# Second cross attention on one core: the next batch's context normalised, and the latent columns scaled, by ScalarE instead of VectorE

## The reference, cut to what matters

```python
def _L1_xattn_ref(x, latents, key_padding_mask, kv_gate, ...):   # x: context (4, 1601, 256), latents (4, 512, 256)
    x = layernorm(x, gamma_media, beta_media)
    latents = layernorm(latents, gamma_lat, beta_lat)
    kv = jnp.concatenate((x, latents * kv_gate), axis=1)         # 2113 rows
    q = (latents @ Wq).reshape(b, n, HEADS, DIM_HEAD)            # 8 heads of 64
    k = (kv @ Wk).reshape(b, f + n, HEADS, DIM_HEAD)
    v = (kv @ Wv).reshape(b, f + n, HEADS, DIM_HEAD)
    sim = jnp.einsum('bqhd,bkhd->bhqk', q * SCALE, k)
    sim = sim - jax.lax.stop_gradient(jnp.max(sim, axis=-1, keepdims=True))
    sim = jnp.where(valid_full[:, None, None, :], sim, NEG_INF)
    attn = jax.nn.softmax(sim, axis=-1)
    out = jnp.einsum('bhqk,bkhd->bqhd', attn, v).reshape(b, n, HEADS * DIM_HEAD)
    return out @ Wout
```

## Time and profile before

| | |
|---|---|
| median of 3 runs | 2505.41 us (2494.01 to 2506.86) |
| the profiled execution's own time | 2506.49 us |
| its span, first to last instruction | 2504.7 us |
| granted TensorE clock, mean over the span | 0.915 |
| busy: TensorE / VectorE / ScalarE / GpSimd | 2048.3 / 1663.0 / 1011.3 / 1016.6 us |

### The profile page before, as it was taken

One profiled execution on the slowest core, in us unless ns is written; L12 is line 12 of the kernel. 1 busy time (PEld: TensorE's weight loads), 2 busy tenths in 40 slices (PEclk: granted clock), 3 DMA queues, 4 the chain that ended last, 5 costly groups with the idle time before them and its releaser, 6 DMA issues. The chain is left out here.

```text
span 2504.7 us, 35270 instructions
## 1 busy us (share of the span) xinstructions
PE 2048.3 (82%) x12728; PEld 1418.6 (57%) x12728; DVE 1663.0 (66%) x2539; ACT 1011.3 (40%) x1662; POOL 1016.6 (41%) x720
## 2 busy tenths in 40 slices
PE   7888857785999944687889888997989997499993
PEld 4555646673344433455556555665656664499992
DVE  5687743343679997489778887888778886422223
ACT  3333210001222210465666566754766674133332
POOL 2232221221344443055456645754566664122221
PEclk9999968897999976789999899998999998699996
DMA  3110044201000000200000000000000000351113
GB/s 143 36 36 20 12 171 158 76 31 59 1 0 0 1 0 3 84 1 1 12 17 1 9 1 27 1 1 9 1 1 1 9 1 1 142 202 35 39 37 109
DMA packets 36455, 93.26 MB, mean 37 GB/s; under 512 B 5160, under 2 KB 24124, under 8 KB 31679
## 3 DMA queue, kind: packets, MB, share of 16 engines
q1 hardware_dynamic: 30206, 74.72, 8.3%
q0 software_dynamic: 6080, 16.29, 1.9%
HBM read 76.56 MB, written 14.44 MB: 36 GB/s over the span
## 5 line engine op out<-in xcount | busy, mean ns | idle before, releaser
L1893 POOL TENSOR_TENSOR x_total<-x_total,x_pt 128x1024 f32<-128x1024 f32 x186 | 438.9, 2360 | 196.9 <-ACT x_pt L1952 180.7
L1973 ACT ACTIVATE x_pt<-PS,x_maskf 128x512 f32<-128x512 f32 x544 | 332.3, 687 | 181.8 <-PE PS L2241 181.4
L2055 DVE TENSOR_TENSOR PS<-x_pt,PS 128x512 f32<-128x512 f32 x480 | 333.2, 694 | 73.7 <-ACT x_pt L1973 36.5
L2212 PE MATMUL PS<-x_pt,x_vs 128*64 128x256 f32 x2176 | 287.9, 406 | 78.3 <-ACT x_pt L1952 72.4
L2073 DVE TENSOR_TENSOR x_pt<-x_pt,PS 128x1024 f32<-128x1024 f32 x320 | 320.5, 1052 | 0.7 <-PE PS L2259 0.7
L1952 ACT ACTIVATE x_pt<-x_pt 128x1536 f32<-128x1536 f32 (+1 forms) x160 | 266.1, 1664 | 50.7 <-DVE x_pt L2073 50.4
L2241 PE MATMUL PS<-x_qs,x_ks 64*128 64x256 f32 x2176 | 281.9, 395 | 1.5 <-ACT x_pt L1973 1.5
L2212 PEld LDWEIGHTS PS<-x_pt,x_vs 128*64 128x64 f32 x2176 | 154.3, 144 | 206.9 <-ACT x_pt L1952 78.4
L1131 PEld LDWEIGHTS PS<-m_xT,m_own 128*128 128x128 f32 x1984 | 235.3, 195 | 9.4 <-DVE m_own L1207 6.4
L1131 PE MATMUL PS<-m_xT,m_own 128*128 128x128 f32 x1984 | 236.3, 278 | 5.1 <-DVE m_own L1207 5.1
L2241 PEld LDWEIGHTS PS<-x_qs,x_ks 64*128 64x128 f32 x2176 | 199.5, 189 | 65.3 <-issue 39.8
(11 more groups left out here) (267 smaller groups left out, 2936.4 us busy)
## 6 DMA issues: line engine op xcount, KB each, us to landing
f_w<-in_L_ffn_w SPq DMA_DIRECT2D x32, 1024.0 KB, 6.9
a_ctxT<-in_ctxT SPq DMA_DIRECT2D x8, 800.5 KB, 4.3
f_w<-ys SPq DMA_DIRECT2D x12, 512.0 KB, 6.4
x_cx<-in_ctx SPq DMA_DIRECT2D x4, 1536.0 KB
l_w<-in_L_attn_w SPq DMA_DIRECT2D x6, 512.0 KB, 6.5
a_xT<-in_xT SPq DMA_DIRECT2D x4, 512.0 KB, 5.2
X<-in_x SPq DMA_DIRECT2D x1, 2048.0 KB, 10.8
xr<-a_xn SPq DMA_DIRECT2D x16, 128.0 KB, 1.7
```

The costliest lines, as they stand in the source:

```text
L1893: ins = nc.gpsimd.tensor_tensor(total2[:], first, tile[:, 2 * k + 2:2 * k + 4, :], ALU.add)
L1973: nc.scalar.activation(pt[:, s % 2, t, :].rearrange("p (h n) -> p h n", h=2), PS[:, first:first + 2, half], ACT.Identity, bias=maskf[:, b ...
L2055: ins = nc.vector.tensor_tensor(acc, tile, acc, ALU.max)
L2212: mm = nc.tensor.matmul(PS[h * HDX:(h + 1) * HDX, AVB, 0:QN], vs[:, p % 2, t, h * HDX:(h + 1) * HDX], pt[:, u % 2, t, h * QN:(h + 1) * QN] ...
```

## The change

- `normalise` for batches 1 to 3 goes from VectorE to ScalarE, in the same slots and groups: 51 instructions. As ScalarE computes scale times input plus a bias, it reads `rs` and a new `shift` = -mean times `rs`. It stands behind the exponent of the group. VectorE still normalises the first batch.
- `gate` goes to ScalarE for all four batches: 8 instructions. It now stands directly behind the move of the last transpose (slot 6, group 4), no longer in slot 7, group 0.
- GpSimd makes `nmu` = -mean (ahead of the power) and `shift` (behind it): two instructions more per batch, 128 x 17 numbers each. The power waits until the previous batch has been normalised.
- VectorE's first statistics of a batch wait for the `shift` of the one before.

The diff:

```diff
@@ rstd on GpSimd
                 nc.gpsimd.tensor_scalar(ve[:], mv[:, :, 1], LN_EPS, None, ALU.add).then_inc(eps_added, 1)
+                nc.gpsimd.tensor_scalar(nmu[:], mv[:, :, 0], -1.0, None, ALU.mult).then_inc(negated, 1)
                 pool.wait_ge(eps_added, b + 1)
+                if b >= 1:
+                    pool.wait_ge(ln_ready, b * NS)
                 nc.gpsimd.tensor_tensor(rs[:], ve[:], g["mhalf"][:].to_broadcast([P, NS]), ALU.pow).then_inc(rs_ready, 1)
+                pool.wait_ge(rs_ready, b + 1)
+                pool.wait_ge(negated, b + 1)
+                nc.gpsimd.tensor_tensor(shift[:], nmu[:], rs[:], ALU.mult).then_inc(shift_ready, 1)
@@ ScalarE
                 ins.then_inc(moved, 1)
+                if use[0] == "N" and use == last_turn(use[1]):
+                    gate(use[1])
+
+            def gate(b):
+                act.wait_ge(moved, MOVED[last_turn(b)])
+                for k in range(KD):
+                    ins = nc.scalar.activation(kvT[:, b % 2, k, S2:KEYS], latT[:, k, :], ACT.Copy, scale=cols[:, 4 * KD:4 * KD + 1])
+                ins.then_inc(gated, 1)
+
+            def normalise(b, i):
+                src, dst, np_ = source(b, i)
+                if i == 0:
+                    act.wait_ge(shift_ready, b + 1)
+                nc.scalar.activation(dst, src, ACT.Identity, bias=shift[0:np_, i:i + 1], scale=rs[0:np_, i:i + 1])\
+                    .then_inc(ln_ready, 1)
...
                     if gi > 0 and exists(s - 1):
                         exponent(s - 1, gi - 1)
+                    if exists(s) and s // UB + 1 < B and s % UB in (3, 4):
+                        at = (s % UB - 3) * NG + gi - 1
+                        for k in (2 * at, 2 * at + 1):
+                            if 0 <= k < NS:
+                                normalise(s // UB + 1, k)
@@ VectorE
                     dve.wait_ge(cx_loaded, 32 * (b + 1))
+                    if b >= 1:
+                        dve.wait_ge(shift_ready, b)
...
-            def gate(b):
-                dve.wait_ge(moved, MOVED[last_turn(b)])
-                for k in range(KD):
-                    ins = nc.vector.tensor_scalar(kvT[:, b % 2, k, S2:KEYS], latT[:, k, :], cols[:, 4 * KD:4 * KD + 1], None, ALU.mult)
-                ins.then_inc(gated, 1)
...
-            dve.wait_ge(w_loaded, 16 * 6)
-            gate(0)
...
-                        if i in (3, 4):
-                            at = (i - 3) * NG + gi - 1
-                            for k in (2 * at, 2 * at + 1):
-                                if 0 <= k < NS:
-                                    normalise(b + 1, k)
-                        if i == UB - 1 and gi == 0:
-                            gate(b + 1)
```

More of the change, by code:

```diff
@@ L1693, in layer1_cross @@
         bn, mv, ve, rs = sb("bn", [P, NS, 6]), sb("mv", [P, NS, 2]), sb("ve", [P, NS]), sb("rs", [P, NS])
+        nmu, shift = sb("nmu", [P, NS]), sb("shift", [P, NS])
         bn2, mv2, ve2, rs2 = sb("bn2", [P, J, 6]), sb("mv2", [P, J, 2]), sb("ve2", [P, J]), sb("rs2", [P, J])
@@ L1713, in layer1_cross @@
         stats_ready, eps_added, rs_ready, ln_ready = sem("stats_ready"), sem("eps_added"), sem("rs_ready"), sem("ln_ready")
-        gated = sem("gated")
+        negated, shift_ready, gated = sem("negated"), sem("shift_ready"), sem("gated")
         chain = sem("chain")
```

## The result

The changed kernel takes 2438.2 us (median of 4 runs, 2431.79 to 2438.73) against 2505.68 us; the ratio is 0.9735 (95% interval 0.9702 to 0.9768), 67 us less. The forecast was 2438, with 95% on faster. Its profiled execution is its fastest, 2431.79 us, and some 4.5 us of that one's 74.7 us of shorter span lie ahead of the slots (the first slot begins at 1038.8 us, before at 1043.2). So the slots are compared one by one.

A forecast was written before the change was run, and what follows sets the result against it. VectorE was taken to bound, or nearly, the slots with normalisations, TensorE the ordinary ones. Terms -53.7 - 22.4 + 6.7 + 1.8 + 0.4 = -67.2 us gave 2438 us; range 2424 to 2464, forecast 2425 to 2450 at 0.75.

The forecast's parts named there:

- The slots without normalisations: Slots 3 and 4 of batches 0 to 2: taking the 51 normalisations off VectorE saves 53.7 us.
- ScalarE's order: Slots 3 and 4, groups 1 to 3: normalisation pairs delay score moves by 0.37 us each, 6.7 us lost.
- Batch 0's comparison: Slots 3 and 4 of batch 0 against two ordinary slots of 28.8 us: 22.4 us saved.
- rival 3: Projections' single bank: pairs delay K or V moves, TensorE idles in 27 groups, clock falls; slower, 2537 at 4 us each; chance 0.02.
- rival 1: ScalarE becomes what the six slots wait for, all its added work shows: 2458 us; chance 0.13.
- Rival 2: Something else holds the slots, say GpSimd's additions meeting output normalisations; half the slots' gain stays away: 2465 us; chance 0.07.
- The gate: Three slots 7: with the gate off VectorE and earlier, they shrink to ordinary odd slots, saving 22.4 us.
- The 1.8 us for ScalarE: Slot 6: the gate on ScalarE delays the last three score moves, costing 0.6 us in each of three batches.
- GpSimd's two instructions: Ahead of the first slot, `nmu` before the power costs 0.4 us; for the other batches it is hidden.
- The price of a normalisation on ScalarE: 128 x 256 with two pointer operands: 0.57 us singly, 0.48 back to back, 24.5 us for all 51.
- signs listed for right: Slots 3 and 4: 63 to 67 us, batch 0 58 to 62; VectorE some 52; slot 7 about 29; normalisations 0.5 to 0.6.
- signs for wrong: K or V projections waiting for ScalarE's moves, normalisations over 1 us, ScalarE waiting for `shift`, slot 6 over 1 us longer.

The follow-up runs named there:

- The run with short additions: Kernel before the change, with GpSimd's additions of the exponents cut to 16 columns of each 512; normalisations and gate stay on VectorE: 2436.81 us in one run.
- The experiment with more work: Changed kernel with a second ScalarE instruction of 128 x 128 ahead of each of its 51 normalisations: 2448.98 us in one run.
- the run with the gate alone: Kernel before the change with only the gate moved to ScalarE, the normalisations staying on VectorE: 2483.46 us, ratio 0.9909.
- the early gate: Kernel before the change with the gate still on VectorE, but at the head of slot 7, ahead of the reduction and four maxima: 2495.91 us, ratio 0.9965.
- either reordering of the pairs: Changed kernel with each normalisation pair one step later in ScalarE's order, 2439.58 us; or slot 4's group 2 pair moved to group 4 in batches 1 and 2, 2435.34 us.

## Why the prediction was right

- **The slots without normalisations** were priced by batch 3 and two ordinary slots, 53.7 us, less 6.7 for ScalarE's order: 47.0. Measured 22.9 + 13.1 + 13.2 = 49.2. The price by comparable slots carried it; by VectorE's 71.7 us the sum would have been 22 us off, by the uncontended 20 us further off on the other side. The run with short additions shows why: in batch 0, 17.8 of 22.9 us go with the additions. (They do not run "all the while": GpSimd is busy 47 of the 80 us.)
- **Batch 0's comparison** was 1.7 us too long. Its slot 4 is an even slot, and an even slot without extra work takes 27.1 us, not 28.8 (slot 0 of batch 3, kernel before):

```profile
1856.10:1883.20 27.10, 26.53 (x207) 18.68 (x205) 23.96 (x31) 20.33 (x28) 17.65 (x9) 1.00 0.01 2
```

  The prediction named this possibility and left it out of the sum.
- **ScalarE's order**, 6.7 us spread evenly over groups of three tiles, was near in size and wrong in place. Against 28.8 + 27.1 us batch 0 shows 1.1 us, batches 1 and 2 show 2.5 and 2.6 over the 63.1 of batch 3: 6.2 in all. In each of the three, four transposes of slot 5 stand ahead of the cut; they take 0.5 us and are no cost of the change, which the comparison had missed. That leaves 4.7, of which 0.5 and 0.6 lie in slots 3 of batches 1 and 2, no more than that slot varies by itself. What can be placed are waits for the single bank: 0.3 us ahead of V projections, 0.4 ahead of a K projection in slot 3, and 1.1 us more ahead of the logits. The pairs do not delay TensorE through the score moves, as the term had it, but where the next use waits for the bank, which was the mechanism of rival 3, at 0.2 us for each of the 27 groups where it needed 3.3. The experiment with more work shows that ScalarE was nonetheless near its limit, which is what rival 1 (2458) lived on.
- **Rival 2** was in part right about what happens: GpSimd's additions do meet the output normalisations at a worse moment (1.37 us before, 4.41 after). It cost the forecast nothing, because batch 3, from which the price was taken, had them at that worse moment already.
- **The gate**, 22.4 us, came out at 22.4 by the slots and 19.6 by the run with the gate alone. That its place on VectorE was not all, the early gate shows. The 1.8 us for ScalarE measured 0.1: slots 6 went from 29.6 to 29.7, since VectorE's reciprocal and the idle time ahead of its reduction covered the rest. Moving the gate of batch 0 cost nothing, as assumed: 25.4 us from the first normalisation to the first slot, with and without it.
- **GpSimd's two instructions**: 0.27 to 0.29 us each for `nmu`, 0.23 for `shift`. The wait of VectorE ahead of the first slot grew from 3.57 to 3.82 us, 0.25 for a predicted 0.4.
- **The price of a normalisation on ScalarE** was worked out from two other forms, with the remark that no row shows the form itself. One does, in another block of the same trace (line, ns min/median/max):

```profile
L1307 ACT ACTIVATE X<-X,c_shift,c_rs x32: 583/585/600, 602.6 to 2500.9; 128x256 f32<-128x256 f32 x32
```

  The remark was wrong, and 0.57 us was 0.02 to 0.04 low. Looked up by shape over the whole trace, the row would have been found.
- **That the median fell on the forecast to 0.2 us is luck.** By the slots the terms give 49.2 + 22.4 - 0.1 - 0.3 = 71.2 us where 67.2 were forecast; the medians differ by 67.5, with an interval from 58 to 75, and the slots that the change leaves alone differ by a few us between the two executions, with the clock. The mechanism and the size are right within some 4 us, no nearer.
- Of the signs listed for right, batch 0 (57.0 us, VectorE 48.0) lay under its bounds and the normalisation (0.61) just over its own; the others came out as listed. One of the signs for wrong came too, in small: a V projection of slot 4 waits 0.32 us for ScalarE's move, and a K projection of slot 3 waits 0.39.

## What to carry to other kernels

Price work taken off an engine by the same stretch without it, in the same trace, and not by the busy time of its instructions: VectorE's 71.7 us were worth 49. Where one engine feeds all the others, small instructions belong on the engine with room whose instructions do not stretch beside GpSimd's, and one that others wait for belongs right behind what it depends on. Work taken off an engine can let its other instructions run into what they had been spared: look at their times too, not only at the one that left. When a wait names an engine that finished 0.6 us before the waiter starts, look for the other semaphore: here what ended 0.1 us before was the cause, and it was worth another 13 us in three slots.

## What the runs showed of the hardware that was not expected

TensorE's low clock comes and goes with the moment, not only with the gaps. Slots 4 and 5 of batch 2 in the second measurement of the changed kernel:

```profile
1655.20:1689.00 33.80, 31.67 (x223) 22.79 (x221) 24.37 (x32) 25.67 (x39) 13.05 (x6) 0.90 0.00 1
1689.00:1727.10 38.10, 34.37 (x218) 21.33 (x216) 24.43 (x31) 25.28 (x35) 21.16 (x11) 0.96 0.00 1
```

In the first measurement the same program's slots 4 and 5 took 30.7 and 36.5 us at a clock of 1.00; here 33.8 and 38.1 at 0.90 and 0.96. One program differs by 5 us over two slots in this way, which is more than either reordering of the pairs gained. What decides in which slot it falls is open; no run here was made to tell.
